# Both attentions of a two-layer kernel: values' products for four heads at once, ScalarE's other work moved behind pairs of exponentials, and TensorE's work spread over the steps

## The reference

```python
# layer 0 (dense)
Qn = Q / max(norm(Q), EPS); Kn = K / max(norm(K), EPS)
attn = softmax(einsum('bhqd,bhkd->bhqk', Qn, Kn) / sqrt(8))
x = x + ga * (gate * einsum('bhqk,bhkd->bhqd', attn, V)) @ Wo.T
# layer 1 (causal)
dots = where(tril, einsum('bhid,bhjd->bhij', q * scale, k), -50000.0)
x = x + ga * einsum('bhij,bhjd->bihd', softmax(dots), v) @ Wo
```

## Time and profile before

| | us |
|---|---|
| median of three executions | 1821.77 |
| the profiled execution, its own time | 1828.18 |
| its span, first to last instruction | 1826.0 |
| dense attention, first to last output product | 100.05 to 529.18 |
| causal attention, first to last output product | 840.55 to 1433.87 |

### The profile page before, as it was taken

One profiled execution on the slowest core, in us unless ns is written; L12 is line 12 of the kernel. 1 busy time (PEld: TensorE's weight loads), 2 busy tenths in 40 slices (PEclk: granted clock), 3 DMA queues, 4 the chain that ended last, 5 costly groups with the idle time before them and its releaser, 6 DMA issues.

```text
span 1826.0 us, 39932 instructions
## 1 busy us (share of the span) xinstructions
PE 1556.5 (85%) x12803; PEld 796.7 (44%) x12803; DVE 1284.0 (70%) x3451; ACT 1188.8 (65%) x2134; POOL 882.6 (48%) x1677
## 2 busy tenths in 40 slices
PE   5799999999967999779999999999999508989970
PEld 3334444444433444324444444444444306777750
DVE  6566777777747888836767677675877536777768
ACT  3777788778756989635565665556555517888860
POOL 6254544545511333324444438747465563555554
PEclk9899999999988999969999999999999558999995
DMA  5221112221208930022211213312221323222228
GB/s 155 75 45 36 36 36 41 42 37 36 47 13 331 386 125 1 23 57 50 48 41 41 46 38 66 69 43 66 45 62 43 112 77 97 75 77 76 76 66 258
DMA packets 238478, 141.20 MB, mean 77 GB/s; under 512 B 184163, under 2 KB 210659, under 8 KB 237253
## 3 DMA queue, kind: packets, MB, share of 16 engines
q1 hardware_dynamic: 227072, 119.72, 24.4%
q0 software_dynamic: 8640, 17.97, 3.0%
q10 hardware_dynamic: 2564, 0.97, 0.2%
HBM read 37.67 MB, written 58.98 MB: 53 GB/s over the span
## 4 chain that ended last, share of the span: by engine, by line
PE 42%; DVE 12%; issue 6%; ACT 2%; DVEq 2%; POOL 2%; DMA 1%; POOLq 1%; SPq 0%; ACTq 0%; another core or an unknown queue 0%
PE OP L2138 8%; PE OP L2003 5%; PE M L2101 5%; PE SP L1983 4%; DVE mx L1329 4%; PE SP L2298 3%; PE SP L2118 2%; PE M L2076 2%; PE M L2097 2%; PE M L2092 2%; PE OP L2313 2%; DVE pt L1620 2%; POOL h_dram L492 1%; PE OP L2150 1%; PE M L1993 1%
## 5 line engine op out<-in xcount | busy, mean ns | idle before, releaser
L863 ACT ACTIVATE pt<-SP 128x768 f32<-128x768 f32 x256 | 207.1, 809 | 250.4 <-PE SP L2118 236.4
L1329 DVE TENSOR_REDUCE mx<-M 128x2 f32<-128x512 f32 (+1 forms) x384 | 258.0, 683 | 104.5 <-PE M L2101 94.6
L531 POOL TENSOR_SCALAR_AFFINE_SELECT pt<-pt 128x256 f32<-128x256 f32 x512 | 198.6, 412 | 262.8 <-ACT pt L863 260.9
L750 ACT ACTIVATE pt<-SP 128x1024 f32<-128x1024 f32 x256 | 255.2, 1019 | 72.1 <-PE SP L1873 72.0
L562 POOL DMA_INDIRECT y_dram<-hT,dest x142 | 140.2, 987 | 134.2 <-DVE hT L1626 112.0
L964 ACT ACTIVATE pt<-SP,b 128x256 f16<-128x256 f32 x284 | 138.2, 487 | 81.8 <-PE SP L2298 81.2
L1892 PE MATMUL OP<-pt,vs 128*32 128x256 f32 x1408 | 186.5, 387 | 0.0
L492 POOL DMA_INDIRECT h_dram<-hT,slot x128 | 130.7, 1021 | 58.8 <-issue 31.7
L2138 PE MATMUL OP<-pt,vs 128*32 128x128 f32 (+1 forms) x1408 | 151.0, 338 | 4.7 <-POOL pt L531 4.7
L1620 DVE TENSOR_TENSOR pt<-vs,pt 128x256 f16<-128x256 f32 x284 | 115.7, 428 | 49.8 <-ACT vs L965 25.0
L656 POOL TENSOR_TENSOR st<-st,ksT 128x512 f32<-128x512 f32 x48 | 72.0, 1500 | 153.1 <-DVE ksT L1751 153.0
(11 more groups left out here) (325 smaller groups left out, 3344.9 us busy)
## 6 DMA issues: line engine op xcount, KB each, us to landing
h_dram<-shared SPq DMA_DIRECT2D x8, 4488.0 KB, 33.5
hT<-h_dram SPq DMA_DIRECT2D x71, 132.0 KB
rows<-g_dram SPq DMA_DIRECT2D x4, 2048.0 KB, 7.1
pt<-y_dram SPq DMA_DIRECT2D x32, 256.0 KB, 3.7
x_sb<-in_x SPq DMA_DIRECT2D x8, 512.0 KB, 8.8
pt<-in_w SPq DMA_DIRECT2D x4, 1024.0 KB
out<-x_sb SPq DMA_DIRECT2D x16, 256.0 KB, 3.0
shared<-st SPq DMA_TRANSPOSE x144, 2.4
```

The lines of the kernel that those rows point to most:

```text
L531: last = pool.affine_select(out=diag, in_=diag, compare_op=ALU.is_ge, fill=0.0, base=0, pattern=[[0, 2], [1, P]], channel_multiplier=-1)
L750: act.activation(pt[:, u % 4], SP[u % 2][:], ACT.Exp, scale=SCALE).then_inc(s["exp"], 1)
L863: act.activation(pt[:, u % 4, :, 0:384], SP[u % 2][:, :, 0:384], ACT.Exp, scale=SCALE).then_inc(s["exp"], 1)
L1329: dve.tensor_reduce(to, M[:, k % 2, :].rearrange("p (j k) -> p j k", j=4 if k < 4 else 2), AX.X, ALU.max).then_inc(s["mred"], 1)
```

## The change

In both attentions `values` takes a pair j of steps: for each key half k it issues the four heads' matmuls one after the other, each in its own strip, where before two heads were finished before the other two began. The same matmuls are issued, to the same places. It waits for the second exponential (or select) of the pair, and raises `pv` by two at its end. It is issued at odd steps, behind the score of step u, for the pair that began three steps earlier.

Dense attention, TensorE: `project`'s halves move from step 1 to steps 2 and 4; `router` goes from step 7 of batch b + 3 to step 2 of batch b + 5; `turn` from step 5 of b + 3 to step 6 of b + 4. ScalarE: `normal` and `enter` work one batch later (b - 4), and the other work stands behind exp 1 (`normal`), exp 3 (`high`), exp 5 (`square`) and exp 7 (`enter`). VectorE's `extra` and `depth` and GpSimd's `low` work on b - 5, and `extra` stands behind `tail_n`. Causal attention, TensorE: the first fill of steps 1, 2 and 4 no longer stands ahead of values, values stands at steps 1, 3, 5 and 7, `enter(b + 3)` goes from step 6 to step 7 ahead of values, `turn3` from step 6 to the end of step 7; VectorE's `tail_t(b - 1, 1)`, `tail_r`, `tail_n` and `tail_a` follow maxima 0, 2, 3, 4 and 5 instead of 2, 4, 5, 6 and 7. The four-slot `pt`, the two SP tiles and all shapes stay.

The core of the diff (dense; the causal `values` changes in the same way):

```diff
                 for b in range(B):
                     exp(b, 0)
                     exp(b, 1)
+                    if b >= 4:
+                        normal(b - 4)
                     exp(b, 2)
                     if b == 0:
                         sigmoid()
+                    exp(b, 3)
                     if b + 2 < B:
                         high(b + 2)
-                    exp(b, 3)
                     exp(b, 4)
+                    exp(b, 5)
                     if b + 3 < B:
                         square(b + 3)
-                    if b >= 3:
-                        normal(b - 3)
-                    exp(b, 5)
                     exp(b, 6)
-                    if b >= 3:
-                        enter(b - 3)
                     exp(b, 7)
+                    if b >= 4:
+                        enter(b - 4)
...
-                def values(b, u):
+                def values(b, j):
...
-                    pe.wait_ge(s["exp"], CH * b + u + 1)
-                    if b and u % 4 == 0:
-                        pe.wait_ge(s["o"], 2 * b + u // 4 - 1)
-                        if u:
+                    pe.wait_ge(s["exp"], CH * b + 2 * j + 2)
+                    if b and j % 2 == 0:
+                        pe.wait_ge(s["o"], 2 * b + j // 2 - 1)
+                        if j:
                             pe.wait_ge(s["wr"], b)
...
                     for k in range(TT):
-                        for i in range(2):
-                            g = 2 * (u % 2) + i
-                            c = (j % 2) * T
+                        for g in range(HG):
                             last = pe.matmul(OP[32 * g:32 * g + 32, j // 2, c:c + T],
                                              vsd[b % 3][:, k, HG * j + g, :],
-                                             pt[:, u % 4, i, k * T:k * T + T],
+                                             pt[:, 2 * (j % 2) + g // 2, g % 2, k * T:k * T + T],
...
-                    last.then_inc(s["pv"], 1)
+                    last.then_inc(s["pv"], 2)
...
                         score(b, u)
...
-                        if CH * b + u >= 2:
-                            values((CH * b + u - 2) // CH, (u - 2) % CH)
-                        if u == 1 and b + 3 < B:
-                            for t in range(TT):
-                                project(b + 3, t)
+                        if u % 2 and CH * b + u >= 3:
+                            values((CH * b + u - 3) // CH, (u - 3) % CH // 2)
+                        if u == 2 and b >= 5:
+                            router(b - 5)
+                        if u in (2, 4) and b + 3 < B:
+                            project(b + 3, u // 2 - 1)
                         if u == 4 and b:
                             tail_wo(b - 1)
-                        if u == 5 and b >= 3:
-                            turn(b - 3)
-                        if u == 7 and b >= 3:
-                            router(b - 3)
+                        if u == 6 and b >= 4:
+                            turn(b - 4)
```

And of the causal attention, VectorE's order and TensorE's loop:

```diff
+                        if b and k == 0:
+                            tail_t(b - 1, 1)
                         if b and k == 2:
-                            tail_t(b - 1, 1)
-                        if b and k == 4:
                             tail_r(b - 1)
-                        if b and k in (5, 6):
-                            tail_n(b - 1, k - 5)
-                        if b and k == 7:
+                        if b and k in (3, 4):
+                            tail_n(b - 1, k - 3)
+                        if b and k == 5:
                             tail_a(b - 1)
...
                         score(b, u)
-                        if FILLS[u] and b + 1 < B:
-                            fill(b + 1, done)
-                            done += 1
-                        if CH * b + u >= 2:
-                            values((CH * b + u - 2) // CH, (u - 2) % CH)
...
-                        for _ in range(FILLS[u] - 1):
-                            if b + 1 < B:
+                        if u == 7 and b + 3 < B:
+                            enter(b + 3)
+                        for n in range(max(FILLS[u], 1)):
+                            if n == (u == 3) and u % 2 and CH * b + u >= 3:
+                                values((CH * b + u - 3) // CH, (u - 3) % CH // 2)
+                            if FILLS[u] and b + 1 < B:
...
-                        if u == 6:
-                            if b + 3 < B:
-                                enter(b + 3)
-                            if b >= 5:
-                                turn3(b - 5)
+                        if u == 7 and b >= 5:
+                            turn3(b - 5)
```

More of the change, by code:

```diff
@@ L638, in dense @@
                         place_v(b + 2)
-                    if b >= 4:
-                        low(b - 4)
+                    if b >= 5:
+                        low(b - 5)
                     if b + 3 < B:
@@ L644, in dense @@
                         weight_low(b - 1)
-                low(B - 4)
                 deviation(B // 2 - 1)
-                for n in range(B - 3, B):
+                for n in range(B - 5, B):
                     low(n)
@@ L785, in dense @@
                         sigmoid()
+                    exp(b, 3)
                     if b + 2 < B:
                         high(b + 2)
-                    exp(b, 3)
                     exp(b, 4)
+                    exp(b, 5)
                     if b + 3 < B:
                         square(b + 3)
-                    if b >= 3:
-                        normal(b - 3)
-                    exp(b, 5)
                     exp(b, 6)
-                    if b >= 3:
-                        enter(b - 3)
                     exp(b, 7)
+                    if b >= 4:
+                        enter(b - 4)
                     if b < CHUNKS:
                         weight_high(0, b)
-                for n in range(B - 3, B):
+                for n in range(B - 4, B):
                     normal(n)
@@ L1273, in dense @@
                 for b in range(B):
-                    if b >= 4:
-                        extra(b - 4)
                     if b == 1:
@@ L1281, in dense @@
                         tail_n(b - 1)
+                    if b >= 5:
+                        extra(b - 5)
                     if b + 2 < B:
@@ L1295, in dense @@
                         tail_x(b - 1)
-                    if b >= 4:
-                        depth(b - 4)
+                    if b >= 5:
+                        depth(b - 5)
                     if b:
@@ L1311, in dense @@
                 variance(B // 2 - 1)
-                for n in range(B - 4, B):
+                for n in range(B - 5, B):
                     extra(n)
@@ L1944, in dense @@
                             pe.wait_ge(gl_in, 1)
-                        if CH * b + u >= 2:
-                            values((CH * b + u - 2) // CH, (u - 2) % CH)
-                        if u == 1 and b + 3 < B:
-                            for t in range(TT):
-                                project(b + 3, t)
+                        if u % 2 and CH * b + u >= 3:
[4 more added lines that the diff above has]
+                            project(b + 3, u // 2 - 1)
                         if u == 4 and b:
                             tail_wo(b - 1)
-                        if u == 5 and b >= 3:
-                            turn(b - 3)
-                        if u == 7 and b >= 3:
-                            router(b - 3)
-                values(B - 1, CH - 2)
-                values(B - 1, CH - 1)
+                        if u == 6 and b >= 4:
+                            turn(b - 4)
+                values(B - 1, NJ - 1)
                 tail_wo(B - 1)
-                for n in range(B - 3, B):
+                router(B - 5)
+                for n in range(B - 4, B):
                     turn(n)
@@ L2121, in score, with values @@
                     last.then_inc(s["score"], 1)
-                def values(b, u):
-                    if u == 0:
+                def values(b, j):
+                    if j == 0:
                         pe.wait_ge(s["vs"], b + 1)
-                    pe.wait_ge(s["sel"], CH * b + u + 1)
-                    if b and u % 4 == 0:
-                        pe.wait_ge(s["o"], 2 * b + u // 4 - 1)
-                        if u:
+                    pe.wait_ge(s["sel"], CH * b + 2 * j + 2)
+                    if b and j % 2 == 0:
+                        pe.wait_ge(s["o"], 2 * b + j // 2 - 1)
+                        if j:
                             pe.wait_ge(s["wr"], b)
-                    j = u // 2
+                    c = (j % 2) * T
                     for k in range(TT):
                         q0 = P if k else 0
-                        for i in range(2):
-                            g = 2 * (u % 2) + i
-                            c = (j % 2) * T
+                        for g in range(HG):
```

(4 more changed lines are left out.)

10 lines of the change are left out of this document (5 added, 5 removed).

## The result

The changed kernel takes 1874.93 us (1872.26 to 1881.75, 4 runs), the kernel before 1823.5 us (1817.3 to 1829.41, 4 runs): a ratio of 1.029 [1.024, 1.034], slower by 51 us. The forecast was 1713, faster by 109. What came is rival D, to which the prediction gave 0.05.

The account below looks back on a forecast made before the run. TensorE was taken to bound both attentions, then VectorE (dense) and a chain through PSUM tile M (causal). Saving 69 and 40 us from 1828.2 gave 1719, less 6.4 for the median 1713; range 1670 to 1765.

Parts of the forecast that it names:

- rival D: Causal attention: TensorE's idle time lowers its clock; 28 us per slow batch, 1878 us with half of them; chance 0.05.
- the 3.76 us ahead of it: Last causal batch of before: TensorE's idle time behind which its clock fell to half, values going from 0.84 to 1.50 us.
- the walk: Step-by-step timing of both attentions' new order: dense pair 1.11 us, causal pair 0.80, periods 11.6 and 17.7.
- Rival E: Dense values: four strips don't run at once, a pair costs 1.98 us, period 13.4 to 13.8, about 1815; chance 0.04.
- VectorE's 11.3 + 0.3: Dense attention: VectorE, the next bound, needs 11.3 us a batch plus 0.3 of waits, saving 69 us.
- rival B: Dense attention: VectorE doesn't run behind TensorE and pays its waits; period 12.4, time 1737; chance 0.16.
- VectorE's waits for L1904's successor: Dense attention: VectorE's waits for TensorE at L1904 were to be gone, as a sign of the forecast being right.
- rival A: Causal attention: the chain through PSUM tile M doesn't get shorter, period stays at 19, time 1753; chance 0.13.
- the circle: Causal attention: dependent chain through PSUM tile M, project to fills, maxima, router, enter, turn3, project; sets a period of 17.7.
- The predicted wait ahead of project: Causal attention: TensorE waits for ScalarE's enter ahead of project, about 0.5 us a period.

Follow-up runs that it names:

- filler_light: Changed kernel plus an added useless 32x32 product by 512 columns ahead of fills 2 to 11 of each causal batch; 1993.01 us, 1.084 of the kernel before.
- pack_filler: Changed kernel with all causal moves undone, packing kept, plus a 128x128 product by 512 columns ahead of causal fills 2 to 11; 1803.73 us, 0.984 of before.
- causal_moves: Changed kernel with causal values made step by step, two heads at once as before, all moves kept; 1871.03 us, 1.030 of the kernel before.
- dense_high: Changed kernel plus 128x128 products ahead of causal fills 2 to 11 (two at 2 and 3), dense `high` behind exponential 4; 1755.22 us, 0.958 of before.
- dense_only: Kernel before with only the dense half of the change, causal attention as before; 1769.51 us, 0.973 of the kernel before.
- dense_again: Kernel before with only the dense half of the change, run once more on another chip; 1785.3 us, 0.974 of the kernel before.
- causal_pack: Changed kernel with all causal moves put back, only the packed values kept there, dense half as changed; 1901.53 us, 1.034 of the kernel before.

## Why the prediction was wrong

**The clock, where it failed.** The prediction saw the mechanism and priced it: it had a causal batch cost 28 us at half clock, and 1878 us with half the batches there. It was all batches, at a mean of 22.85, since each has some 7 us at full clock. That 1878 stands beside the measured 1875 is luck: half the batches at 28 cost what all of them at 22.85 do. The step that failed is the argument for the chance of 0.05: "the single gaps I find are 0.6 us and less, and gaps of that size stand in today's stretches at full clock". The gaps were as found (0.49, 0.56, 0.20), and before does stand still for 0.60 us (1075.88) at full clock; the conclusion doesn't follow: filler_light loses the clock with no gap at all, and pack_filler holds it across one of 1.12 us. What the change altered was what stands between the gaps. A pair of values' steps went from 1.54 us to 0.79 (977.58 to 978.37), so the stretch of fills and scores, of 24 and 32 rows, came together. I had counted what TensorE saves as time gained; the same 3 us were also work that had helped to keep the array loaded. They weren't all of it: with them back and the moves kept (causal_moves) the clock is 0.81 over the causal attention, so the moves lose it in a way of their own, which stays open. Once down, the clock stays down for the rest of the batch, with TensorE still for only 0.2 us in 17, and comes back at the batch's end, in values or in the 128x128 products there, of which project is the longest. The trace of before did show a batch at half clock with hardly a gap in it; the prediction put that down to the 3.76 us ahead of it, and did not ask why the clock stayed low behind it.

**Values.** 16 records were expected in about 1.2 us; they take 1.07 in the dense half and 0.86 in the causal one. From start to next start the dense pair takes 1.02 (300.01 to 301.03), where the walk took 1.11 from two steps back to back, and the causal one 0.79, where it took 0.80. Rival E is out.

```profile
300.01 1.07 PE L1889 MATMUL OP<-pt,shared 128*32 128x256 f32 x16
```

**The dense period.** 11.6 expected, 12.19 measured: -51 us and not -69. That TensorE is no longer the bound was right; the mis-sized term is "VectorE's 11.3 + 0.3". ScalarE sets the pace, with a wait for VectorE in its row that the walk didn't have:

```profile
307.58 1.98 ACT L749 ACTIVATE pt<-SP 128x1024 f32<-128x1024 f32 x2
311.54 0.63 ACT L739 ACTIVATE st<-qkv 128x512 f16<-128x512 f32 x1 [1.98 <-DVE qkv L1164]
```

Its busy time is 322.81 / 31 = 10.4 us a period; its waits for unit over 252 to 450 are 14.4 + 10.3 us in 16 batches, 1.5; those for scores 3.6 us, 0.2. The sum is 12.2. dense_high bears the term out in part: an exponential in the wait takes 0.6 us off it, but only 0.3 off the period, so the row of ScalarE alone doesn't set the pace; unit comes later when ScalarE is earlier. What that circle allows stays open. The predicted total lies near rival B's 12.4, by another wait than B's. That VectorE's waits for L1904's successor would vanish was right: 0.3 us in 198. A further part varies: the same kernel has its dense attention in 373.3 us at clock 0.97 (dense_only) and 380.9 at 0.91 (dense_again), so the clock dips here too; at 0.97 the period is 12.04.

**The causal period.** 17.7 expected at full clock. No run shows it without added work; with it 18.59, of which TensorE is busy 17.63, 2.1 of that the added products. So rival A (the circle isn't shorter) is out, by 0.6 us at least, and whether the circle alone would allow 17.7 stays open. The predicted wait ahead of project, about 0.5 us, is there: 0.39. Two readings of the walk were off: TensorE isn't busy for 0.87 us of before's period (19.19 less 18.32), not 0.4, and the output products around the four routed parts are 22.1, 26.4, 21.8 and 17.5 us apart, not 26.4 each time.

**Behind the causal attention** the changed kernel took 370.5 us and the kernel before 392.1, for which no step of the prediction speaks, nor does the change: the same kernel shows both, dense_only 370.8 and dense_again 389.7. Thirty us of that stretch in each:

```profile
1608.09:1638.09 30.00, 29.14 (x370) 24.53 (x369) 24.38 (x87) 27.09 (x73) 18.12 (x19) 1.00 0.28 83
...
1598.16:1628.16 30.00, 27.70 (x346) 22.86 (x343) 22.32 (x79) 25.58 (x69) 16.84 (x18) 1.00 0.27 81
```

The clock is 1.00 in both and TensorE gets through 370 and 346 matmuls. It goes with the chip, or with the hour, since the experiments of a chip ran together: the stretch takes 370.3 to 371.9 us in the four experiments on dense_only's chip and 389.0 to 390.9 in the eight on the three others. What differs there is open, and on which the profiled executions of before and after ran isn't on record. So the -21.7 us of this stretch can't be put down to the change.

## What to carry to other kernels

Where products use few of the array's rows or columns, time saved on TensorE can cost its clock: before packing or closing up such a stretch, find what keeps the clock at full (here the longer values' products were part of it), and expect the loss even if no gap grows. Test it with one cheap run, the same kernel with full 128x128 products in the thin stretch: if adding work shortens the period, the clock was the bound. And walk every engine's row for waits on the others when the first bound is taken away: ScalarE's own sum was 10.4 us of a period of 12.2. Compare two profiled executions by stage, at like clock and on one chip: here 20 us between chips and 7 us between clocks of one stage would have passed for effects.

## What the runs showed of the hardware

TensorE's granted clock was 0.63 over a stretch in which it was busy for 99.8% of the time, with 24-, 32-row and 32x32 products, and 1.00 over the same row of products with ten 128x128 products in place of the 32x32 ones. From start to next start a 128x128 product by 512 columns took 0.23 us, a 32x32 one 0.32, at full clock. Twice as many thin records side by side (16 in 0.86 us) lowered the clock, too: causal_pack at 0.64 against dense_only at 1.00, the packing being the only difference in that half. At half clock a group's time, from first start to last end, is not doubled: 1.51 us for 0.86 (sixteen records of the values), 0.39 for 0.28 (the 256-column mask), 2.93 for 1.89 (project; 2.93 in the changed kernel at 904.71, wholly at half clock).
